# Where the router's features of a recurrence stage are made: VectorE, or ScalarE and GpSimd

## The chip, the cores and the metric

One NeuronCore of one Trainium2 chip runs the whole program. The metric is the device time of one execution in microseconds, lower is better. Before the change it is 8120.26 us (median of three runs, 8118.91 to 8121.44).

Names of engines as in the profile: PE is TensorE (PEld its weight loads), DVE is VectorE, ACT is ScalarE, POOL is GpSimd, SP is SyncE with its DMA queue.

## What is computed

Four layers are applied to x of shape (2, 4096, 512), each added to its input: a state-space layer, a dense layer, a gated linear recurrence with 8 heads of 64, and a routed spline layer. Only the third and the start of the fourth matter here:

```python
# third layer: decaying state per head
state = (1.0 - w_t)[..., :, None] * state + k_t[..., :, None] * v_t[..., None, :]
out = einsum('bhd,bhde->bhe', r_t, state)
x3 = x + out @ Wo.T

# fourth layer: norms twice, then routes by signs
z  = layernorm(x3)
xf = (z - mean(z)) * rsqrt(var(z) + 1e-5) * ln_gamma + ln_beta
tile_scores = sign(xf) @ tile_sigs.T       # 64 tiles of 8 features, in 8 clusters
tile_idx    = argmax over the tiles of the best cluster
x_slice     = the 8 values of xf that belong to tile_idx
```

Both norms together are one: with m the mean of x3 and s the joint factor, xf = (x3 - m) * s * gamma + beta. These xf, one row of 512 per token, are called the features below.

## The kernel before

All is in float32. Five stages follow one another: `pre_phase`, `scan_phase`, `mid_phase`, `core_phase`, `final_phase`. The change touches `core_phase` alone, the recurrence stage. It works through 64 items of 128 tokens (32 for each of the two sequences, taken in alternation: `par` is the sequence, `m` the place in it). Within an item the recurrence is done in parallel form: sub-blocks of 8 tokens, joined in a tree of four levels.

Each engine has its own program, a list of pieces run by `pipelined`. In one turn t an engine runs each piece of its list once, in the order of the list, for item t + lead. Engines keep no common clock; they are held together by `Count` semaphores: `c.inc(ins)` counts a finished instruction of an item, `c.wait(eng, item, n)` waits until n of that item are done, `c.wait_all` until all are. No planner orders anything: the lists are the order. For the turn of lead 1 (item i = t + 1) they are:

- DVE (L1349): `state` (L1270: four state updates; L1276: x3 = x + y from PSUM), `norms` (L1280 to L1286: mean, variance, ve), `limits` (L1348, item t), `centred` (L1292, L1295: the factors rt, by a Newton step on POOL's root; L1297, L1298: the features), `decays` (L1312, L1314: sixteen products for item t + 4, each of an SBUF operand with one in PSUM), `route` (L1333 to L1340: scores, best tile, one-hot oh), `spread_scores` (L1325, item t + 3).
- POOL (L1238): `more_keys` (item t + 3), `root` (L1160: ve to the power -0.5), `last_keys` (t + 3: L1175, L1183 twice, then L1219 twice, kl and ql), `totals` (L1167), `flip` (L1230: signs times the tiles' signs), `keys` (L1191 to L1183, item t + 4, waits for `decays`), `pick` (L1236: features times one-hot).
- ACT (L1417): `own_reads` (L1370, L1371, item t + 4), `pad_keys` (L1378), `attended` (L1385: two copies ats; L1387: k8t; item t + 2), `scores` (L1396, item t + 3), `kept` (L1403 to L1406: the layer's output x3 + z into xo), `signs` (L1412), `outputs` (L1416, item t + 2).
- PE (L1520): `tree` (L1460, item t + 2, waits for `spread_scores`), `turn_keys` (L1468), `products` (L1479, item t + 3), `reads` (L1489, L1495), `turn_scores` (L1502), `sums` (L1512), `outputs` (L1518).
- SP (L1139): loads of a, k, r five items ahead, of v and x three ahead, and the store of xo.

The features have one buffer, xf [128, 512]. They are written by DVE, read by ACT for the signs and by POOL in `pick`:

```python
after.link(dve, dve.scalar_tensor_tensor(out=xf[:], in0=x3[:], scalar=mv[:, 0:1], in1=gam[:], op0=ALU.subtract, op1=ALU.mult))
after.inc(dve.scalar_tensor_tensor(out=xf[:], in0=xf[:], scalar=rt[:, 1:2], in1=bet[:], op0=ALU.mult, op1=ALU.add))
```

Chain for one item: DVE `norms`, POOL `root`, DVE `centred`, ACT `signs`, POOL `flip`, DVE `route`, POOL `pick`, DVE `limits` one turn later.

Of the kernel before, what the change touches and what calls it, by code (L numbers as in the profile page):

```python
# [3 lines left out]
ALU = mybir.AluOpType  # L4
# [984 lines left out]
def core_phase(nc, D, H, L, a_s, k_s, r_s, v_s, x2_s, wo_d, gam_d, bet_d, slopes_d, key_row_d, mask_d, hmask_d, ident_d, x3_s, oh_out, xs_out):  # L989
# [15 lines left out]
    with ExitStack() as ctx:  # L1005
# [27 lines left out]
        mask = sb("mask", [P, P]); hmask = sb("hmask", [P, P]); ident = sb("ident", [P, P]); heads = sb("heads", [P, 2, P // 8])  # L1033
        st = sb("st", [P, 6]); mv = sb("mv", [P, 2]); ve = sb("ve", [P, 2]); half_neg = sb("half_neg", [P, 2]); r0 = sb("r0", [P, 2]); rt = sb("rt", [P, 2]); tmp = sb("tmp", [P, 2]); nve = sb("nve", [P, 2])
        keep = sb("keep", [P, 2])
# [31 lines left out]

        act_a = Count(sem("act_a"), 4)

        after = Count(sem("after"), 17)  # L1070
        S_STATE, S_X3, S_VE, S_RT, S_XF, S_OH = 1, 2, 6, 11, 13, 17

        pool_b = Count(sem("pool_b"), 3)

        routed = Count(sem("routed"), 1)

        act_r = Count(sem("act_r"), 5)
        R_KEPT = 4

# [68 lines left out]
        def _(pool):  # L1148
# [5 lines left out]
            pool.wait_ge(zeroed, 7)  # L1154
            pool.wait_ge(sgn_ready, 1)

            def root(i, par, m):
# [54 lines left out]
            def last_keys(i, par, m):  # L1212
                last = 8
                for l in range(3, LEVELS):
                    last = wider(i, par, l, last)
                pool_a.wait(pool, i, last)
                for kind, src, dst in ((1, rk[:, par, SUB], steps(kl[:, par])), (0, first[:, par, 0:SUB], ql[:, par])):
                    f = far[LEVELS][:, kind * C:(kind + 1) * C].rearrange("p (o c) -> p o c", o=1).broadcast_to([P, SUB, C])
                    pool_a.inc(pool.tensor_tensor(dst, src, f, ALU.mult))  # L1219

            def totals(i, par, m):
                totaled.begin(i)

                after.wait(pool, i - 2, S_STATE)
                totaled.inc(join(LEVELS - 1, par))

            def flip(i, par, m):
# [4 lines left out]
            def pick(i, par, m):  # L1232
# [4 lines left out]
                                              oh[:, bass.ds(par * (L // P) + m, 1), :].rearrange("p o (n e) -> p (o n) e", e=1).broadcast_to([P, NT, 8]), ALU.mult))  # L1237
            pipelined(pool, ITEMS, [(3, more_keys), (1, root), (3, last_keys), (3, totals), (1, flip), (4, keys), (1, pick)])  # L1238

        @block.vector  # L1240
        def _(dve):
# [46 lines left out]
            def centred(i, par, m):  # L1288
                pool_b.wait(dve, i, 1)
                after.wait(dve, i, S_VE + 1)  # L1290
                for e in range(2):
                    after.inc(dve.tensor_scalar(tmp[:, e:e + 1], r0[:, e:e + 1], r0[:, e:e + 1], nve[:, e:e + 1], ALU.mult, ALU.mult))  # L1292
                after.wait(dve, i, S_VE + 3)
                for e in range(2):
                    after.inc(dve.tensor_scalar(rt[:, e:e + 1], tmp[:, e:e + 1], 1.5, r0[:, e:e + 1], ALU.add, ALU.mult))  # L1295
                after.wait(dve, i, S_RT)
                after.link(dve, dve.scalar_tensor_tensor(out=xf[:], in0=x3[:], scalar=mv[:, 0:1], in1=gam[:], op0=ALU.subtract, op1=ALU.mult))  # L1297
                after.inc(dve.scalar_tensor_tensor(out=xf[:], in0=xf[:], scalar=rt[:, 1:2], in1=bet[:], op0=ALU.mult, op1=ALU.add))  # L1298

# [17 lines left out]
            def spread_scores(i, par, m):  # L1317
                spread.begin(i)
                pe_a.wait_all(dve, i)

                act_a.wait(dve, i - 1, 2)
                shape = [P, Q, NI, SUB]
# [6 lines left out]
            def route(i, par, m):  # L1329
                at = lambda t: t[:, bass.ds(par * (L // P) + m, 1), :].rearrange("p o n -> p (o n)")  # L1330

                pool_b.wait(dve, i, 2)
                dve.tensor_reduce(ts[:], sg[:], AX.X, ALU.add).then_inc(key_read, 1)  # L1333
# [18 lines left out]
        def _(act):  # L1352
# [27 lines left out]
            def attended(i, par, m):  # L1380
                act_a.begin(i)

                pe_b.wait(act, i, B_TREE)
                for h2 in range(2):
                    act_a.inc(act.copy(ats[:, h2], at_ps[:, h2]))  # L1385
                pe_b.wait(act, i, B_KEYS)
                act_a.inc(act.copy(k8t[:], kt_ps))  # L1387

# [8 lines left out]

            def kept(i, par, m):
                act_r.begin(i)

                act.wait_ge(x3_out[par], (m + 1) * 16)
                after.wait(act, i, S_RT)
                act_r.inc(act.activation(keep[:, 0:1], rt[:, 0:1], ACT.Identity, bias=1.0))  # L1403
# [4 lines left out]
            def signs(i, par, m):  # L1408

                after.wait(act, i, S_XF)  # L1410
                act.wait_ge(key_read, i + 1)
                act_r.inc(act.activation(signs_of, by_tile(xf), ACT.Sign))  # L1412

            def outputs(i, par, m):
                pe_b.wait(act, i, B_OUT)
                act_a.inc(act.copy(ot[:], o_ps))  # L1416
            pipelined(act, ITEMS, [(4, own_reads), (3, pad_keys), (2, attended), (3, scores), (1, kept), (1, signs), (2, outputs)])  # L1417

        @block.tensor
        def _(pe):  # L1420
# [62 lines left out]
            def reads(i, par, m):  # L1483

                pool_a.wait_all(pe, i)
                after.wait(pe, i - 2, S_STATE)
                act_a.wait(pe, i, 3)
                for q in range(Q):
                    pe.matmul(o_ps[:, q, :], s[:, par, q, :], steps(ql[:, par, :, q * NI:(q + 1) * NI]), start=(q == 0), stop=True, skip_group_check=True)  # L1489
                act_a.wait(pe, i, 2)  # L1490
                pe.wait_ge(ins_b[par], (m + 1) * 32)
# [13 lines left out]
            def sums(i, par, m):  # L1505

                act_a.wait(pe, i, 3)
                after.wait(pe, i - 1, S_STATE)
# [300 lines left out]
```

## Time and profile before

| what | value |
|---|---|
| median of three runs | 8120.26 us (8118.91 to 8121.44) |
| the profiled execution | 8123.72 us |
| its span in the profile | 8121.9 us |
| busy over the span | PE 7231.2 (89%), DVE 6749.7 (83%), ACT 4754.7 (59%), POOL 5820.1 (72%) |
| L1297 and L1298, 64 each | first features at 6722.8 us, last at 7868.0 us |

The profile is of one execution. Its times count from the span's start. In a timeline each line has the start, the duration, the engine, the line of the program, the operation with output <- inputs, and in brackets how long the engine sat idle before it and which instruction ended that. Durations contain the tail of an instruction, which the next one on the same engine overlaps by some 0.05 us. PEclk is the granted share of TensorE's full clock.

### The profile page before, as it was taken

To read this page: it belongs to the slowest core of one execution; us is meant where nothing else is said; L and a number is where in the kernel's file an instruction comes from. 1 tells how busy PE (TensorE), PEld (TensorE's weight loads), DVE (VectorE), ACT (ScalarE), POOL (GpSimd) and SP (SyncE) were. 2 spreads that over 40 slices of the span, in tenths; PEclk is the share of its full clock that TensorE was granted. 3 is DMA by queue.
4 is the path that set the end of the run, shared out by engine and by line. 5 is a ranking of instruction groups with operands and counts; after the bars stand their busy time and mean duration, and the time that the engine had idled before them with its cause. 6 is when DMAs were issued, how large, how long until landed. Compare 5 with 4: busy or idle time off the path is not lost. (4 is left out here: it accounts for less than half of the span.)

```text
span 8121.9 us, 217686 instructions
## 1 busy us (share of the span) xinstructions
PE 7231.2 (89%) x74510; PEld 5288.9 (65%) x74510; DVE 6749.7 (83%) x8153; ACT 4754.7 (59%) x10889; POOL 5820.1 (72%) x3400
## 2 busy tenths in 40 slices
PE   8799999999999999999999999799999988888863
PEld 4577777777777777777777777444444435555542
DVE  7799999999999999999999999423232329999976
ACT  7778778778887787888877877211111113333320
POOL 1499999999999999999999999300000006777644
PEclk9999999999999999999999999899999998888875
DMA  6500000000000000000000000212211222222224
GB/s 208 157 1 16 16 8 8 16 13 4 16 16 0 16 16 0 16 16 0 17 16 0 16 5 0 81 74 92 88 72 72 93 77 88 88 85 86 86 84 155
DMA packets 198187, 389.94 MB, mean 48 GB/s; under 512 B 26224, under 2 KB 51888, under 8 KB 186544
## 3 DMA queue, kind: packets, MB, share of 16 engines
q1 hardware_dynamic: 189088, 370.45, 13.7%
q10 hardware_dynamic: 8976, 17.83, 0.6%
q8 instruction: 80, 1.31, 0.1%
q14 instruction: 43, 0.35, 0.0%
HBM read 208.52 MB, written 179.70 MB: 48 GB/s over the span
## 5 line engine op out<-in xcount | busy, mean ns | idle before, releaser
L494 POOL TENSOR_TENSOR scan_hc<-scan_h,scan_cb 128x1024 f32<-128x1024 f32 x2048 | 4776.3, 2367 | 103.0 <-PE scan_y L617 81.7
L659 DVE TENSOR_TENSOR_SCAN scan_h<-scan_a,scan_carry,scan_u 128x512 f32<-128x512 f32 x4096 | 4800.3, 1256 | 15.8 <-PE scan_u L606 8.0
L553 ACT ACTIVATE scan_a<-scan_dt,scan_aneg 128x512 f32<-128x512 f32 x4096 | 2658.3, 708 | 7.4 <-ACT scan_yo L533 7.4
L606 PE MATMUL scan_u<-scan_dg,scan_v 64*128 64x128 f32 x32768 | 2379.8, 285 | 313.3 <-DVE scan_h L659 269.5
L606 PEld LDWEIGHTS scan_u<-scan_dg,scan_v 64*128 64x128 f32 x32768 | 1990.4, 187 | 793.2 <-DVE scan_h L659 556.2
L617 PE MATMUL scan_y<-scan_ident,scan_hc 128*128 128x128 f32 x16408 | 2251.8, 280 | 14.3 <-ACT scan_yo L533 9.9
L617 PEld LDWEIGHTS scan_y<-scan_ident,scan_hc 128*128 128x128 f32 x16408 | 1758.2, 140 | 272.9 <-ACT scan_yo L533 15.7
L524 ACT ACTIVATE scan_dg<-scan_half,scan_bt 128x64 f32<-128x64 f32 x4096 | 1139.0, 341 | 5.9 <-DVE scan_onward L645 5.2
L164 POOL TENSOR_TENSOR mid_r<-mid_ve,mid_half_neg 128x4 f32<-128x4 f32 x32 | 32.4, 1012 | 1288.0 <-DVE mid_ve L132 797.7
L545 ACT ACTIVATE scan_carry<-scan_h,scan_onward 128x4 f32 (+1 forms) x1008 | 302.9, 300 | 934.3 <-DVE scan_h L659 934.2
L809 DVE TENSOR_TENSOR mid_x<-mid_x,mid_pa 128x512 f32<-128x512 f32 x64 | 44.1, 688 | 432.8 <-PE mid_pa L918 432.8
L865 ACT ACTIVATE mid_rt<-mid_pb 128x512 f32<-128x512 f32 x64 | 38.2, 598 | 610.1 <-PE mid_pb L929 610.1
L798 DVE TENSOR_TENSOR mid_x<-mid_x,mid_pa 128x512 f32<-128x512 f32 x64 | 44.0, 688 | 318.3 <-PE mid_pa L900 318.3
L1385 ACT COPY core_ats<-core_at_ps 128x512 f32<-128x512 f32 x128 | 68.7, 590 | 397.3 <-PE core_at_ps L1460 397.3
L1460 PE MATMUL core_at_ps<-core_first,core_rk 64*8 64x8 f32 x4096 | 90.8, 174 | 201.5 <-DVE core_at_ps L1325 197.0
L1314 DVE TENSOR_TENSOR core_rk<-core_rr,core_ak_ps 128x128 f32<-128x128 f32 (+7 forms) x512 | 260.3, 508 | 0.0
L860 ACT ACTIVATE mid_at<-mid_pb,mid_bwn 128x512 f32<-128x512 f32 x64 | 44.0, 687 | 345.3 <-PE mid_pb L929 320.4
L929 PE MATMUL mid_pb<-mid_xnt,mid_wr 128*128 128x512 f32 x512 | 223.9, 595 | 20.7 <-DVE mid_kt L821 20.7
L1518 PE MATMUL core_y_ps<-core_wo,core_ot 128*128 128x512 f32 x512 | 236.8, 605 | 0.2 <-ACT core_ot L1416 0.2
L1460 PEld LDWEIGHTS core_at_ps<-core_first,core_rk 64*8 64x8 f32 x4096 | 70.9, 91 | 252.1 <-issue 252.1
L826 DVE COPY mid_vv<-mid_pb 128x512 f32<-128x512 f32 x64 | 44.3, 692 | 227.0 <-PE mid_pb L954 227.0
L1312 DVE TENSOR_TENSOR core_rr<-core_rr,core_ak_ps 128x128 f32<-128x128 f32 (+6 forms) x448 | 212.9, 475 | 20.1 <-ACT core_rr L1371 10.7
(212 smaller groups left out, 7246.5 us busy)
## 6 DMA issues: line engine op xcount, KB each, us to landing
scratch_y<-scan_yo ACTq DMA_DIRECT2D x17, 1024.0 KB, 4.3
pre_x<-in_x SPq DMA_DIRECT2D x16, 1024.0 KB, 5.7
scratch_dt<-pre_dt SPq DMA_DIRECT2D x16, 1024.0 KB, 5.8
scratch_vr<-pre_vr SPq DMA_DIRECT2D x16, 1024.0 KB, 4.7
scan_dt<-scratch_dt SPq DMA_DIRECT2D x16, 1024.0 KB, 5.3
scan_v<-scratch_vr SPq DMA_DIRECT2D x32, 512.0 KB, 7.6
mid_yr<-scratch_y SPq DMA_DIRECT2D x16, 1024.0 KB, 7.0
mid_x<-in_x SPq DMA_DIRECT2D x16, 1024.0 KB, 8.2
```

Source lines behind the costliest of these rows:

```text
L494: pool.tensor_tensor(hc[:, q].rearrange("p n (r j) -> p n r j", j=P), h[:, q].rearrange("p n (r j) -> p n r j", j=P), cb[:, bass.ds(b * NS ...
L524: last = act.activation(dg[:, buf, k, :, n], half[:], ACT.Identity, scale=bt[:, par, k, bass.ds(first + n, 1)])
L545: act.activation(carry[:, q0:q0 + 2, bass.ds(first, 2)], h[:, q0:q0 + 2, :, T - 1], ACT.Identity, scale=keep[:, bass.ds(c, 1)]).then_inc(s ...
L553: ins = act.activation(a[:, q, n, :], dt[:, par, q, :], ACT.Exp, scale=aneg[:, q, bass.ds(m * 2 + n, 1)])
L606: mm = pe.matmul(u_ps[:, q % 2, g, k * HP:(k + 1) * HP, :], v[row, par, k, q, :], dg[row, buf, k], start=True, stop=True)
L617: mm = pe.matmul(y_ps[:, j, q * P:(q + 1) * P], hc[:, q, n, j * P:(j + 1) * P], ident[:], is_transpose=True, start=first and n == 0, stop= ...
L659: ins = dve.tensor_tensor_scan(h[:, q, n, :], a[:, q, n, :], u_ps[:, q % 2, :, :, n].rearrange("p g t -> p (g t)"), carry[:, q, bass.ds(m ...
L929: mm = pe.matmul(pb[:, o, :], weight[:, q, o * P:(o + 1) * P], src[:, q, :], start=(q == 0), stop=(q == Q - 1))
L1312: decayed = chain.inc(dve.tensor_tensor((rr[:, j - 1] if j else first[:, par])[:, j:W], rr[:, j, j:W], ak_ps[:, 0, j:j + 1, :].broadcast_t ...
L1314: chain.inc(dve.tensor_tensor(rk[:, par, j:W, j, :], rr[:, j, j:W], ak_ps[:, 1, j:j + 1, :].broadcast_to(shape), ALU.mult))
L1460: mm = pe.matmul(at_ps[lo:lo + rows, h2, q, at + n:at + 2 * n], keys, reads, start=False, stop=True, skip_group_check=True, tile_position= ...
L1518: mm = pe.matmul(y_ps[:], ot[:, q, :], wo[:, q, :], start=(q == 0), stop=(q == Q - 1))
```

## The change

The features are made in three steps on two engines: ACT computes (x3 - m) * s as an activation with scale s and bias `shift` = -m * s; POOL multiplies by gam and adds bet, both in place. DVE makes only `shift`. On POOL the new piece `features` stands between `last_keys` and the two products of L1219, which become a piece of their own, `ends_keys`. On ACT the new piece `normed` stands ahead of `attended`, and `attended` copies k8t first. `signs` waits for POOL in place of DVE. POOL also waits once, at the stage's start, for the constants. Counts and waits are renumbered.

```diff
-        after = Count(sem("after"), 17)
-        S_STATE, S_X3, S_VE, S_RT, S_XF, S_OH = 1, 2, 6, 11, 13, 17
-        pool_b = Count(sem("pool_b"), 3)
+        A_K8T, A_ATS = 1, 3
+        after = Count(sem("after"), 16)
+        S_STATE, S_X3, S_VE, S_RT, S_SHIFT, S_OH = 1, 2, 6, 11, 12, 16
+        pool_b = Count(sem("pool_b"), 5)
+        B_XF, B_FLIP = 3, 4
-        act_r = Count(sem("act_r"), 5)
-        R_KEPT = 4
+        act_r = Count(sem("act_r"), 6)
+        R_XN, R_KEPT = 1, 5
...
             def last_keys(i, par, m):
                 last = 8
                 for l in range(3, LEVELS):
                     last = wider(i, par, l, last)
-                pool_a.wait(pool, i, last)
+
+            def ends_keys(i, par, m):
+                pool_a.wait(pool, i, A_TREE - 2)
                 for kind, src, dst in (...):
...
+            def features(i, par, m):
+                act_r.wait(pool, i, R_XN)
+                pool_b.inc(pool.tensor_tensor(xf[:], xf[:], gam[:], ALU.mult))
+                pool_b.wait(pool, i, B_XF - 1)
+                pool_b.inc(pool.tensor_tensor(xf[:], xf[:], bet[:], ALU.add))
...
-            pipelined(pool, ITEMS, [(3, more_keys), (1, root), (3, last_keys), (3, totals), (1, flip), (4, keys), (1, pick)])
+            pipelined(pool, ITEMS, [(3, more_keys), (1, root), (3, last_keys), (1, features), (3, ends_keys), (3, totals), (1, flip), (4, keys), (1, pick)])
...
                 after.wait(dve, i, S_RT)
-                after.link(dve, dve.scalar_tensor_tensor(out=xf[:], in0=x3[:], scalar=mv[:, 0:1], in1=gam[:], op0=ALU.subtract, op1=ALU.mult))
-                after.inc(dve.scalar_tensor_tensor(out=xf[:], in0=xf[:], scalar=rt[:, 1:2], in1=bet[:], op0=ALU.mult, op1=ALU.add))
+                after.inc(dve.tensor_scalar(shift[:], mv[:, 0:1], rt[:, 1:2], -1.0, ALU.mult, ALU.mult))
...
             def attended(i, par, m):
                 act_a.begin(i)
-                pe_b.wait(act, i, B_TREE)
+                pe_b.wait(act, i, B_KEYS)
+                act_a.inc(act.copy(k8t[:], kt_ps))
                 for h2 in range(2):
                     act_a.inc(act.copy(ats[:, h2], at_ps[:, h2]))
-                pe_b.wait(act, i, B_KEYS)
-                act_a.inc(act.copy(k8t[:], kt_ps))
...
+            def normed(i, par, m):
+                act_r.begin(i)
+                pool_b.wait_all(act, i - 1)
+                after.wait(act, i, S_SHIFT)
+                act_r.inc(act.activation(xf[:], x3[:], ACT.Identity, bias=shift[:], scale=rt[:, 1:2]))
+
             def kept(i, par, m):
-                act_r.begin(i)
                 act.wait_ge(x3_out[par], (m + 1) * 16)
-                after.wait(act, i, S_RT)
...
             def signs(i, par, m):
-                after.wait(act, i, S_XF)
+                pool_b.wait(act, i, B_XF)
...
-            pipelined(act, ITEMS, [(4, own_reads), (3, pad_keys), (2, attended), (3, scores), (1, kept), (1, signs), (2, outputs)])
+            pipelined(act, ITEMS, [(4, own_reads), (3, pad_keys), (1, normed), (2, attended), (3, scores), (1, kept), (1, signs), (2, outputs)])
```

## Rows read from the trace of the kernel before

**Rows 1.** Busy time by stretch: mid stage, then recurrence stage; columns in the header.

```profile
core 0: us, PE busy (x) PEld busy (x) DVE busy (x) ACT busy (x) POOL busy (x), PEclk, DMA share, GB/s
5900.00:6100.00 200.00, 194.25 (x534) 91.48 (x533) 57.04 (x124) 29.36 (x47) 17.91 (x8) 1.00 0.20 73
7000.00:7300.00 300.00, 244.17 (x5104) 166.50 (x5104) 287.49 (x657) 113.62 (x247) 209.08 (x311) 0.87 0.26 85
```

**Rows 2.** Timeline of DVE, one turn: start us, us, engine, line, operation [idle before].

```profile
7192.31 1.11 DVE L1270 SCALAR_TENSOR_TENSOR core_s<-core_s,core_total,core_su_ps 128x128 f32<-128x128 f32 x4
...
7196.77 0.34 DVE L1295 TENSOR_SCALAR core_rt<-core_tmp,core_r 128x1 f32<-128x1 f32 x2
7197.14 1.25 DVE L1297 SCALAR_TENSOR_TENSOR core_xf<-core_x,core_mv,core_gam 128x512 f32<-128x512 f32 x1
7198.43 1.65 DVE L1298 SCALAR_TENSOR_TENSOR core_xf<-core_xf,core_rt,core_bet 128x512 f32<-128x512 f32 x1
7200.00 0.28 DVE L1312 TENSOR_TENSOR core_rr<-core_rr,core_ak_ps 128x128 f32<-128x128 f32 x1
...
7206.90 0.74 DVE L1333 TENSOR_REDUCE core_ts<-core_sg 128x64 f32<-128x576 f32 x1
...
7210.55 1.11 DVE L1270 SCALAR_TENSOR_TENSOR core_s<-core_s,core_total,core_su_ps 128x128 f32<-128x128 f32 x4
```

**Rows 3.** Timeline of POOL, the same turn.

```profile
7197.12 0.72 POOL L1183 TENSOR_TENSOR core_qr<-core_first,core_far 128x256 f32<-128x256 f32 x1
7197.81 1.73 POOL L1219 TENSOR_TENSOR core_kl<-core_rk,core_far 128x512 f32<-128x512 f32 x1
7199.49 1.73 POOL L1219 TENSOR_TENSOR core_ql<-core_first,core_far 128x512 f32<-128x512 f32 x1
7201.18 0.20 POOL L1167 TENSOR_TENSOR core_total<-core_joint 128x4 f32<-128x4 f32 x1
7201.62 1.20 POOL L1230 TENSOR_TENSOR core_sg<-core_sg,core_sgn 128x512 f32<-128x512 f32 x1 [0.25 <-ACT core_sg L1412]
7207.14 0.30 POOL L1191 COPY core_own<-core_first 128x64 f32<-128x64 f32 x1 [4.32 <-DVE core_rk L1314]
...
7209.92 1.08 POOL L1236 TENSOR_TENSOR core_pr<-core_xf,core_oh 128x512 f32<-128x512 f32 x1
```

**Rows 4.** Timeline of ACT, the same turn.

```profile
7196.60 1.07 ACT L1385 COPY core_ats<-core_at_ps 128x512 f32<-128x512 f32 x2 [5.87 <-PE core_at_ps L1460]
...
7200.21 0.82 ACT L1406 ACTIVATE core_xo<-core_x,core_keep 128x512 f32<-128x512 f32 x1
7200.93 0.62 ACT L1412 ACTIVATE core_sg<-core_xf 128x512 f32<-128x512 f32 x1
```

**Rows 5.** Timeline of POOL, then DVE, in the stage's first turn.

```profile
6725.75 1.28 POOL L1219 TENSOR_TENSOR core_ql<-core_first,core_far 128x512 f32<-128x512 f32 x1
...
6731.17 1.20 POOL L1230 TENSOR_TENSOR core_sg<-core_sg,core_sgn 128x512 f32<-128x512 f32 x1 [3.98 <-ACT core_sg L1412]
...
6735.74 1.11 DVE L1270 SCALAR_TENSOR_TENSOR core_s<-core_s,core_total,core_su_ps 128x128 f32<-128x128 f32 x4
```

**Rows 6.** Two lines' instructions: count, ns min/median/max, first and last start.

```profile
L1219 POOL TENSOR_TENSOR core_kl<-core_rk,core_far x64: 1273/1730/1747, 6696.4 to 7837.0; 128x512 f32<-128x512 f32 x64
...
L1297 DVE SCALAR_TENSOR_TENSOR core_xf<-core_x,core_mv,core_gam x64: 750/1253/1265, 6722.8 to 7868.0; 128x512 f32<-128x512 f32 x64
```

**Rows 7.** Timeline of DVE: first and last of 60 turn starts.

```profile
6754.36 1.11 DVE L1270 SCALAR_TENSOR_TENSOR core_s<-core_s,core_total,core_su_ps 128x128 f32<-128x128 f32 x4
...
7831.02 1.11 DVE L1270 SCALAR_TENSOR_TENSOR core_s<-core_s,core_total,core_su_ps 128x128 f32<-128x128 f32 x4
```

**Rows 8.** Timeline of PE, a turn with a stretch at the lower clock.

```profile
7265.64 0.37 PE L1460 MATMUL core_at_ps<-core_first,core_rk 64*8 64x8 f32 x16 [3.67 <-DVE core_at_ps L1325]
...
7269.75 1.12 PE L1468 MATMUL core_y_ps<-core_ident,core_kl 128*128 128x128 f32 x4
...
7277.65 3.70 PE L1518 MATMUL core_y_ps<-core_wo,core_ot 128*128 128x512 f32 x8
```

More of the change, by code:

```diff
@@ L1033, in core_phase @@
         mask = sb("mask", [P, P]); hmask = sb("hmask", [P, P]); ident = sb("ident", [P, P]); heads = sb("heads", [P, 2, P // 8])
-        st = sb("st", [P, 6]); mv = sb("mv", [P, 2]); ve = sb("ve", [P, 2]); half_neg = sb("half_neg", [P, 2]); r0 = sb("r0", [P, 2]); rt = sb("rt", [P, 2]); tmp = sb("tmp", [P, 2]); nve = sb("nve", [P, 2])
+        st = sb("st", [P, 6]); mv = sb("mv", [P, 2]); ve = sb("ve", [P, 2]); half_neg = sb("half_neg", [P, 2]); r0 = sb("r0", [P, 2]); rt = sb("rt", [P, 2]); tmp = sb("tmp", [P, 2]); nve = sb("nve", [P, 2]); shift = sb("shift", [P, 1])
         keep = sb("keep", [P, 2])
@@ L1155, in _ @@
             pool.wait_ge(sgn_ready, 1)
+            pool.wait_ge(consts, 128)
             def root(i, par, m):
@@ L1319, in spread_scores @@
                 pe_a.wait_all(dve, i)
-                act_a.wait(dve, i - 1, 2)
+                act_a.wait(dve, i - 1, A_ATS)
                 shape = [P, Q, NI, SUB]
@@ L1330, in route @@
                 at = lambda t: t[:, bass.ds(par * (L // P) + m, 1), :].rearrange("p o n -> p (o n)")
-                pool_b.wait(dve, i, 2)
+                pool_b.wait(dve, i, B_FLIP)
                 dve.tensor_reduce(ts[:], sg[:], AX.X, ALU.add).then_inc(key_read, 1)
@@ L1486, in reads @@
                 after.wait(pe, i - 2, S_STATE)
-                act_a.wait(pe, i, 3)
+                act_a.wait(pe, i, A_K8T)
                 for q in range(Q):
                     pe.matmul(o_ps[:, q, :], s[:, par, q, :], steps(ql[:, par, :, q * NI:(q + 1) * NI]), start=(q == 0), stop=True, skip_group_check=True)
-                act_a.wait(pe, i, 2)
+                act_a.wait(pe, i, A_ATS)
                 pe.wait_ge(ins_b[par], (m + 1) * 32)
@@ L1505, in sums @@
             def sums(i, par, m):
-                act_a.wait(pe, i, 3)
+                act_a.wait(pe, i, A_K8T)
                 after.wait(pe, i - 1, S_STATE)
```

## The prediction

> **What bounds the kernel now.** I read the windows of busy time first, then the timelines of DVE, POOL and ACT over one turn, then the forms of single lines. The recurrence stage (features from 6722.8 to 7868.0 [rows 6]) is some 1,150 of the 8,122 us; in it DVE is busy 287.49 of 300 us, PE 244, POOL 209 and ACT 114 [rows 1]. The reader should see one engine without room and three with some. DVE's timeline shows the same: from 7192.31 to 7210.55 its instructions follow one another [rows 2]. So a turn lasts as long as DVE's list. From 6754.36 to 7831.02 there are 59 turns of 18.25 us [rows 7]: that is P, and 0.1 us of P is worth 5.9 us. I count the parts of a turn from DVE's first instruction of it, 7192.31 = 0: the features begin at 4.83 (L1297) and 6.12 (L1298), the sixteen multiplications of `decays` at 7.69, `route` at 14.59 (L1333), and the next turn at 18.24 [rows 2].
>
> POOL in the same turn is idle for 4.32 us before L1191 [rows 3]. Its two 128x512 key products (L1219) last 1.73 us each, just beside DVE's two feature instructions. Yet the shortest of that line is 1.273 us, and one in the first turn, begun after the features, took 1.28 [rows 5, 6]. DVE's L1297 likewise takes 1.25 us but at its shortest 0.75 [rows 2, 6]. So these pairs hold each other up: the 0.46 us that each key product has over 1.27 is the features' doing.
>
> **Part 1: off DVE.** L1297 and L1298 go: 4.83 to 7.69, 2.86 us. One 128x1 product for `shift` comes in; two of that size take 0.34 us [rows 2], so 0.20, to 5.03. The multiplications then begin at 5.03, last 6.90 (7200.00 to 7206.90) and end at 11.93.
>
> **Part 2: onto ACT.** The activation has the form of L1406, a 128x512 Identity with bias and scale from tiles: 0.82 us [rows 4]. A handoff costs 0.07 (L1412 ends at 7201.55, L1230 begins at 7201.62) [rows 3, 4]. It runs from 5.10 to 5.92. Its other waits, for `pick` of the item before, ended a turn earlier. Behind it on ACT stand `attended`, `scores`, `kept` and `signs`, now from 7196.60 to 7201.55, 4.95 us or 4.29 to 9.24 [rows 4]. They begin 1.6 later, when the activation is done and PE has turned the keys (5.2, at the lower clock about 5.5 [rows 8]); so the signs are ready by 10.9. Of `attended` the copy k8t now comes first. PE's `reads` want it first as well, and the two ats copies (1.07 us [rows 4]) only for their second half, so I cost the swap at nothing; without that cover PE would lose at most the 0.6 of one copy, out of the slack of part 4.
>
> **Part 3: onto POOL.** Two 128x512 products. The trace before has none with two plain rows; the nearest are L1236, 1.08 us, and L1230, 1.20, and above them L1219 beside DVE, 1.73 [rows 3]. I take L1230's 1.20, since its two inputs are full rows too. POOL has finished L1183 at 5.53 and idles until ACT's result: first product 5.99 to 7.19, handoff 0.07, second 7.26 to 8.46. The key products follow: they have no feature instruction beside them any more, so 1.27 each less 0.05 overlap, to 10.90. The total's product (0.20 [rows 3]) and a handoff put `flip` at about 11.2, just behind the signs. The new wait of `features` delays only the key products, which PE wants a turn later.
>
> **Part 4: what is late next.** `flip` takes 1.20 and then `route` can begin: 12.45, half a microsecond after the multiplications are over (11.93). DVE waits 0.5 there. What comes after `flip` is read in the first turn, where DVE waited for it as well: `flip` began at 6731.17 and the next turn at 6735.74, 4.57 us later [rows 5]. So P = 11.2 + 4.57 = 15.77. POOL's rest of the turn (L1191 to L1236 and `more_keys`) keeps its distance to the turn's start, because there too it began right behind `flip`; so the next `root` finds POOL free as now. PE is busy 244.17 x 18.25 / 300 = 14.9 us per turn [rows 1]; a long one, with a stretch at the lower clock, goes from 7265.64 to 7281.35, 15.7 [rows 8]. It starts 0.3 after DVE's turn does (7265.64 against 6754.36 + 28 x 18.25), so it ends at 16.0 at worst and its next turn begins at 16.1. It fits, barely. Its tree, 4.1 us of that (to 7269.75), ends at 4.4, before the multiplications, which wait for it, begin at 5.03. The change issues and moves no DMA; the loads and the store of a turn stay the same, so their 85 GB/s and 0.26 share [rows 1] grow by 18.25 / 15.77 to 98 GB/s and 0.30, which I cost at nothing: they are issued three and five items ahead. The norm ahead of the features is as before: DVE's `norms`, POOL's `root`, which finds POOL idle, and DVE's L1292 and L1295.
>
> **Sum.** 59 turns x (18.25 - 15.77) = 146.3 us off. The turn before them, 6735.74 to 6754.36 [rows 5, 7], was partly held by PE: I count half, 1.3 off. In the last turn nothing hides the longer way from shift to signs: 0.20 + 0.82 + 2 x 1.20 + three handoffs = 3.6 in place of 2 x 0.75 [rows 6], 2.1 on. Net 145.5. The profiled execution took 8123.7 (span 8121.9, 1.8 around it), so 7978.2 for it; the median of the runs shown, 8120.3, is 3.4 lower: **7975 us**. Bounds: products at 1.08 give P 15.53 (7961), at 1.73 P 16.83 (8037). The floor is DVE without any wait: 11.93, plus 3.27 from `route` to the next turn (4.57 less 1.20 and a handoff of 0.1), P 15.20, or 7941.
>
> **The clock.** At 97% busy in the mid stage TensorE had 1.00 of its clock, at 81% here 0.87, a mix of the 2.4 and 1.2 GHz levels [rows 1]. In the new turn PE would be busy over 90% of the time, so I expect the share to rise. It is worth nothing to the sum while PE has slack.
>
> **Rivals.** *DVE stays the bound*: products at 1.08 or overlapped better, no wait at `route`; P 15.2 to 15.5, 7941 to 7959. Against it: POOL's chain must lose 0.5 us. *The lock moves, it does not go*: the key products stay at 1.73 because something else of DVE's holds them up, P + 0.92 = 16.69, 8029. For it: the 1.73 is nearly constant. Against: the 1.28 of the first turn fell beside the multiplications [rows 5]. The Trainium skill (Perfetto Trace Analysis, Optimizing Scalar/DVE Operations) speaks against the change as a whole: VectorE and GpSimd share an SBUF read port, so moving work between those two might not help. By that rule this rival is the likely one; I keep it low for the row of 1.28. Its page SBUF — State Buffer (Who interferes with whom) narrows it: a VectorE instruction with two SBUF inputs and a GpSimd instruction that reads SBUF block each other fully. The 0.46 us agree; and since the multiplications read one operand from PSUM, by this rule my main case holds.
>
> *PE becomes the bound*: the stretches at the lower clock stay and every turn is the long one, P 16.1, 7994. *Slower than before*: POOL's four large products (4.9 us in a row, 5.99 to 10.90) hold up DVE's multiplications, which start at the same time. Fully blocked, these end at 16.83, P = 20.1, 8230. It decides from 3.05 us of blocking per turn on (18.25 - 15.20). Against it: the first of them, 0.28 us from 7200.00, runs wholly beside an L1219 that ends at 7201.22 and does not wait for it [rows 2, 3]. *The wait takes all*: the way over three engines costs 2.4 more than I add up, and the time is as before.
>
> **How the numbers follow.** Main case 0.68, DVE bound 0.12, lock moved 0.08, PE bound 0.06, as before 0.03, slower 0.03. The prediction is the main case. The range runs from the floor, 7941, to the lock's rival, 8030; it takes in PE's and all but the highest price of the products. A measurement of this kernel tells 0.2%, 16 us, from no change. Faster 0.94, same 0.03, slower 0.03.
>
> **What would show it.** In the profile after: DVE idle about 0.5 us before L1333's reduction, released by POOL's `flip`; L1219 at 1.27; two new POOL groups at about 1.2; POOL waiting some 0.4 for ACT's activation; turn starts 15.8 apart; a granted clock over 0.9. I am wrong if L1219 stays at 1.7, if L1312 and L1314 grow, or if DVE waits for PE at L1312 or L1325.

## The result and the profile after

| | before | after |
|---|---|---|
| median, four runs each on one chip | 8119.59 us (8112.90 to 8121.44) | 7977.44 us (7975.57 to 7979.41) |
| ratio | | 0.9827 [0.9815, 0.9838] |
| profiled execution, its span | 8123.72, 8121.9 us | 7975.57, 7973.8 us |
| turn of the recurrence stage | 18.25 us | 15.845 us |
| busy in the span: DVE, POOL | 6749.7, 5820.1 us | 6579.7, 5927.6 us |
| granted clock, whole span | 0.957 | 0.966 |

The change is faster by 142.2 us; forecast were 145. The second stretch of [rows 1], 7000 to 7300, after the change (same columns):

```profile
7000.00:7300.00 300.00, 277.68 (x6003) 187.90 (x6003) 278.82 (x740) 138.93 (x303) 274.64 (x399) 0.93 0.30 99
```

DVE is down from 287.49 to 278.82 us, POOL up from 209 to 274.64, PE up from 244 to 277.68: three engines are now at 91 to 93%. The granted clock is up from 0.87 to 0.93. One turn on DVE, to be held against [rows 2]:

```profile
7191.33 1.11 DVE L1283 SCALAR_TENSOR_TENSOR core_s<-core_s,core_total,core_su_ps 128x128 f32<-128x128 f32 x4
...
7195.75 0.34 DVE L1308 TENSOR_SCALAR core_rt<-core_tmp,core_r 128x1 f32<-128x1 f32 x2
7196.12 0.21 DVE L1310 TENSOR_SCALAR core_shift<-core_mv,core_rt 128x1 f32<-128x1 f32 x1
7196.60 0.29 DVE L1324 TENSOR_TENSOR core_rr<-core_rr,core_ak_ps 128x128 f32<-128x128 f32 x1 [0.26 <-issue]
...
7202.84 0.75 DVE L1326 TENSOR_TENSOR core_rk<-core_rr,core_ak_ps 128x576 f32<-128x576 f32 x1
7203.80 0.75 DVE L1345 TENSOR_REDUCE core_ts<-core_sg 128x64 f32<-128x576 f32 x1 [0.21 <-POOL core_sg L1243]
...
7204.84 0.45 DVE L1349 SCALAR_TENSOR_TENSOR core_key<-core_cl,core_ts 128x64 f32<-128x64 f32 x1
...
7205.69 0.36 DVE L1352 TENSOR_SCALAR core_oh<-core_key,core_kmax 128x64 f32 x1 [0.15 <-DVE core_kmax L1351]
...
7207.17 1.11 DVE L1283 SCALAR_TENSOR_TENSOR core_s<-core_s,core_total,core_su_ps 128x128 f32<-128x128 f32 x4
```

The same turn on POOL, against [rows 3]:

```profile
7196.15 0.73 POOL L1186 TENSOR_TENSOR core_qr<-core_first,core_far 128x256 f32<-128x256 f32 x1
7197.26 1.28 POOL L1236 TENSOR_TENSOR core_xf<-core_xf,core_gam 128x512 f32<-128x512 f32 x1 [0.38 <-ACT core_xf L1414]
7198.62 1.28 POOL L1238 TENSOR_TENSOR core_xf<-core_xf,core_bet 128x512 f32<-128x512 f32 x1
7199.86 1.30 POOL L1225 TENSOR_TENSOR core_kl<-core_rk,core_far 128x512 f32<-128x512 f32 x1
7201.11 1.27 POOL L1225 TENSOR_TENSOR core_ql<-core_first,core_far 128x512 f32<-128x512 f32 x1
...
7202.50 1.19 POOL L1243 TENSOR_TENSOR core_sg<-core_sg,core_sgn 128x512 f32<-128x512 f32 x1
7203.76 0.29 POOL L1194 COPY core_own<-core_first 128x64 f32<-128x64 f32 x1
...
7204.35 0.85 POOL L1186 TENSOR_TENSOR core_kc<-core_rk,core_own 128x256 f32<-128x256 f32 x1
```

and on ACT, against [rows 4]:

```profile
7196.37 0.81 ACT L1414 ACTIVATE core_xf<-core_x,core_shift,core_rt 128x512 f32<-128x512 f32 x1 [6.62 <-DVE core_shift L1310]
...
7200.66 0.64 ACT L1428 ACTIVATE core_sg<-core_xf 128x512 f32<-128x512 f32 x1
```

All key products of the stage (count, ns min/median/max), against [rows 6]:

```profile
L1225 POOL TENSOR_TENSOR core_kl<-core_rk,core_far x64: 1272/1292/1309, 6691.2 to 7691.0; 128x512 f32<-128x512 f32 x64
```

Counted from the turn's start at 7191.33: the activation runs from 5.04 to 5.85, the first product begins at 5.93, `flip` at 11.17, DVE's `route` at 12.47 after 0.21 us idle, and the next turn at 15.84. The key products take 1.29 us where they took 1.73. Two things were not on my list. DVE stands idle 0.26 us before its first multiplication (7196.60), with no engine named. And the key of `route` (L1349; L1337 before) takes 0.45 us where it took longer before:

```profile
7207.92 0.74 DVE L1337 SCALAR_TENSOR_TENSOR core_key<-core_cl,core_ts 128x64 f32<-128x64 f32 x1
```

**Where the 148.1 us between the two spans are.** 58 turns (6763.52 to 7682.51) at 15.845 in place of 18.25: 139.4. The three before them took 18.88, 17.54 and 16.76 us, against 19.01, 18.62 and 18.25: 2.7 (before the change DVE began the stage's first turn at 6716.73; the starts of the next two are in [rows 5, 7]). The end of the program from the last long turn on is 0.4 us longer. That leaves 6.4 us: the stage's first turn began at 6710.34 in place of 6716.73, before anything that was changed, and repeated runs of one kernel differ by as much (6716.34 in the changed kernel's second profile, below). The first turns gained little because DVE waited for PE's tree, 1.56 us in the first turn and 1.18 in the third. PE had begun that first tree 2.76 us after DVE began the turn (6713.10), where it is 0.32 to 0.35 in later turns. From 6680 to 6702, while PE was mostly idle or waiting, its granted clock was 0.50, the 1.2 GHz level; from 6706 to 6714 it was 1.00. How much of the delay is the clock's, no run shows. DVE in the first turn after the change:

```profile
6710.34 1.11 DVE L1283 SCALAR_TENSOR_TENSOR core_s<-core_s,core_total,core_su_ps 128x128 f32<-128x128 f32 x4
...
6718.65 0.29 DVE L1324 TENSOR_TENSOR core_rr<-core_rr,core_ak_ps 128x128 f32<-128x128 f32 x1 [1.56 <-PE core_at_ps L1476]
...
6729.22 1.11 DVE L1283 SCALAR_TENSOR_TENSOR core_s<-core_s,core_total,core_su_ps 128x128 f32<-128x128 f32 x4
```

### The profile page after: what moved, and what is told of

The parts are those of the page before. It is cut to its first block and busy times, and to the rows that moved or that the text cites. A ratio compares the mean times of both kernels' runs of the same rounds, so it can differ in the third digit from the quotient of the medians.

```text
span 7973.8 us, 217784 instructions
## 1 busy us (share of the span) xinstructions
PE 7210.3 (90%) x74510; PEld 5270.5 (66%) x74510; DVE 6579.7 (83%) x8089; ACT 4783.8 (60%) x10953; POOL 5927.6 (74%) x3528
## 5 line engine op out<-in xcount | busy, mean ns | idle before, releaser
L617 PEld LDWEIGHTS scan_y<-scan_ident,scan_hc 128*128 128x128 f32 x16408 | 1757.4, 140 | 272.9 <-ACT scan_yo L533 15.7
L1414 ACT ACTIVATE core_xf<-core_x,core_shift,core_rt 128x512 f32<-128x512 f32 x64 | 52.1, 814 | 425.4 <-DVE core_shift L1310 425.4
L1326 DVE TENSOR_TENSOR core_rk<-core_rr,core_ak_ps 128x128 f32<-128x128 f32 (+7 forms) x512 | 263.4, 514 | 0.0
L1324 DVE TENSOR_TENSOR core_rr<-core_rr,core_ak_ps 128x128 f32<-128x128 f32 (+6 forms) x448 | 215.9, 482 | 38.0 <-PE core_at_ps L1476 12.6
L929 PE MATMUL mid_pb<-mid_xnt,mid_wxw 128*128 128x512 f32 x512 | 225.7, 594 | 0.9 <-DVE mid_vv L826 0.9
L918 PE MATMUL mid_pa<-mid_w,mid_ht 128*128 128x512 f32 x512 | 224.1, 596 | 2.1 <-ACT mid_ht L852 2.1
```

What stands on the lines that cost most here:

```text
L617: mm = pe.matmul(y_ps[:, j, q * P:(q + 1) * P], hc[:, q, n, j * P:(j + 1) * P], ident[:], is_transpose=True, start=first and n == 0, stop= ...
L918: mm = pe.matmul(pa[:, j, :], ht[:, q, j * P:(j + 1) * P], w["w0"][:, q, :], start=(q == 0), stop=(q == Q - 1))
L929: mm = pe.matmul(pb[:, o, :], weight[:, q, o * P:(o + 1) * P], src[:, q, :], start=(q == 0), stop=(q == Q - 1))
L1324: decayed = chain.inc(dve.tensor_tensor((rr[:, j - 1] if j else first[:, par])[:, j:W], rr[:, j, j:W], ak_ps[:, 0, j:j + 1, :].broadcast_t ...
L1326: chain.inc(dve.tensor_tensor(rk[:, par, j:W, j, :], rr[:, j, j:W], ak_ps[:, 1, j:j + 1, :].broadcast_to(shape), ALU.mult))
```

## The experiments

Twelve kernels ran, each beside the kernel before on the same chip; the text calls them by the first part of their names (e1, e2 and so on). Unless it says otherwise, a diff is against the changed kernel. "Turn" is the mean over some 30 turns of the profile. The changed kernel, run again as the yardstick:

> The changed kernel once more, as the yardstick for the runs beside it: ratio to the kernel before 0.982 to 0.983, turn 15.84 us.

Measured: 7980.86 us (7977.19 to 7982.98), ratio 0.9828 [0.9815, 0.9842], turn 15.844.

### What the features cost DVE before: work or waiting?

e1: in the kernel before, the two feature instructions are replaced by two reductions that read the same row of x with one input.

```diff
-                after.link(dve, dve.scalar_tensor_tensor(out=xf[:], in0=x3[:], scalar=mv[:, 0:1], in1=gam[:], ...))
-                after.inc(dve.scalar_tensor_tensor(out=xf[:], in0=xf[:], scalar=rt[:, 1:2], in1=bet[:], ...))
+                after.link(dve, dve.bn_stats(st_a[:], x3[:]))
+                after.inc(dve.bn_stats(st_b[:], x3[:]))
```

> The kernel before, with DVE's two feature instructions (two SBUF inputs each, 1.25 and 1.65 us) replaced by two BATCH_NORM_STATS of x3 (one SBUF input each, 0.69 us); the features are left out. My theory, that the two features and POOL's two key products hold each other up: the key products (L1219 before) fall from 1.73 to about 1.27 us each although POOL's list is untouched, the two reductions fill 0.85 + 0.65 = 1.5 us of DVE's turn in place of 2.86, and the turn falls from 18.25 to 16.9 us, some 80 us in all. So 1.36 of the 2.86 us that the change took off DVE were waiting for the port. Rival (the key products are slow by themselves or because of DVE's multiplications): they stay at 1.7.

Measured: 8030.89 us (two runs), ratio 0.9892 [0.9863, 0.992], turn 16.73. POOL's key products in it:

```profile
L1219 POOL TENSOR_TENSOR core_kl<-core_rk,core_far x64: 1274/1288/1308, 6694.4 to 7744.3; 128x512 f32<-128x512 f32 x64
```

1.29 us, with POOL's own list untouched. So the two engines did hold each other up. On DVE the two reductions fill 1.34 us, and the turn is 1.52 shorter. The shortest of the two feature instructions take 0.75 us each, 1.5 together, so of their 2.86 us some 1.36 were waiting. The reductions have one input less, but they also write only six elements per partition; e1 by itself does not tell these two apart. The multiplications do: they write full rows to SBUF with one input in SBUF and one in PSUM, and they take no longer beside POOL's products (below, under the other rivals).

### One product less, one more

e2: without the second of the two products.

```diff
-                pool_b.wait(pool, i, B_XF - 1)
-                pool_b.inc(pool.tensor_tensor(xf[:], xf[:], bet[:], ALU.add))
```

> The changed kernel, without the addition of bet on POOL (left out of the computation). My theory: POOL's chain from the activation to flip sets the turn, but only by DVE's 0.22 us idle before route; with one product (1.36 us with its handoff) less, DVE's own list sets it: turn 15.84 - 0.22 = 15.6 us, some 13 us less in all, DVE's idle before route gone. Rival (POOL is the bound throughout): turn 14.5 us, 80 us less.

Measured: 7977.94 us (two runs), ratio 0.9826 [0.9798, 0.9855], turn 15.85: nothing gained. DVE in `route`:

```profile
7189.72 0.74 DVE L1343 TENSOR_REDUCE core_ts<-core_sg 128x64 f32<-128x576 f32 x1
...
7190.75 0.75 DVE L1347 SCALAR_TENSOR_TENSOR core_key<-core_cl,core_ts 128x64 f32<-128x64 f32 x1
...
7191.92 0.35 DVE L1350 TENSOR_SCALAR core_oh<-core_key,core_kmax 128x64 f32 x1 [0.17 <-DVE core_kmax L1349]
```

DVE's idle before L1343, the first line, is gone as forecast, but the key after it (L1347) is at 0.75 us again, where the changed kernel had 0.45. What the end of the wait gave, the key took. POOL in the same turn:

```profile
7189.96 0.30 POOL L1194 COPY core_own<-core_first 128x64 f32<-128x64 f32 x1 [1.17 <-DVE core_rk L1324]
...
7190.57 0.85 POOL L1186 TENSOR_TENSOR core_kc<-core_rk,core_own 128x256 f32<-128x256 f32 x1
```

POOL's piece `keys`, which waits for DVE's last multiplication, now waits for it openly. In the changed kernel `keys` (L1194, 7203.76) begins 0.17 us after the end of the last multiplication (L1326, 7203.59), the same distance as here, in e7 and before the change. So there too the multiplications released it, although `flip` had ended only 0.07 us before. In both kernels L1186 begins 13.02 to 13.03 us into the turn, and that is why they have the same turn.

e3: a third product, by a row of ones, is put in.

```diff
                 pool_b.inc(pool.tensor_tensor(xf[:], xf[:], bet[:], ALU.add))
+                pool_b.wait(pool, i, B_XF - 1)
+                pool_b.inc(pool.tensor_tensor(xf[:], xf[:], ones_row[:], ALU.mult))
```

> The changed kernel, with a third product of the same size on the features on POOL (by a row of ones). My theory: it lies wholly on the chain that sets the turn: turn 15.84 + 1.28 + 0.08 = 17.2 us, 80 us more than the changed kernel, and all of it as DVE's idle time before route (0.22 becomes 1.6). Rival (PE or DVE sets the turn and POOL has room): less than half of that.

Measured: 8059.85 us, ratio 0.9924 [0.9902, 0.9947], turn 17.12, 1.28 more. The first instruction of `route`:

```profile
7197.65 0.75 DVE L1348 TENSOR_REDUCE core_ts<-core_sg 128x64 f32<-128x576 f32 x1 [1.53 <-POOL core_sg L1245]
```

A product more costs 1.28 us, one less gives nothing: the changed kernel stands within 0.1 us of where the two ways to POOL's `keys`, over `flip` and over the multiplications, are equally long. In e3, e5, e6 and e9 `flip` is the last of the two, and the next turn then begins 4.55 to 4.57 us after its start; in the changed kernel it is 4.67.

### The order on ACT and on POOL

e4: the order of ACT's copies alone, in the kernel before (k8t ahead of ats, counts renumbered as in the change):

> The kernel before, with ACT's attended in the changed order alone (k8t ahead of the two ats copies). My theory: worth nothing by itself, since DVE's list sets the turn: turn 18.25 us, within 5 us of the kernel before. Rival (part of the 2.41 us per turn comes from this order, through PE's reads): faster by over 16 us.

Measured: 8118.92 us against 8118.03, ratio 1.0001 [0.9992, 1.001], turn 18.26. It is worth nothing by itself.

e5: the activation stands behind `attended` and `scores`.

```diff
-            pipelined(act, ITEMS, [..., (1, normed), (2, attended), (3, scores), (1, kept), (1, signs), (2, outputs)])
+            pipelined(act, ITEMS, [..., (2, attended), (3, scores), (1, normed), (1, kept), (1, signs), (2, outputs)])
```

> The changed kernel, with normed moved on ACT from ahead of attended to its old place, just ahead of kept. My theory: the activation then starts only after the scores' copies, 7.6 us after the turn's start in place of 5.04; POOL waits with nothing else to do, since its list is in order, and the turn grows by all of it: about 18.3 us, some 150 us more than the changed kernel, no faster than the kernel before. Rival (the place on ACT doesn't matter because POOL's key products or DVE's multiplications cover it): within 20 us of the changed kernel.

Measured: 8130.25 us, ratio 1.0014 [1.0002, 1.0025], turn 18.20. The activation's place in ACT's list is worth the whole gain: with the work moved off DVE all the same, the kernel is no faster than before.

e6: the key products stand ahead of the features on POOL.

```diff
-            pipelined(pool, ITEMS, [..., (3, last_keys), (1, features), (3, ends_keys), (3, totals), (1, flip), ...])
+            pipelined(pool, ITEMS, [..., (3, last_keys), (3, ends_keys), (1, features), (3, totals), (1, flip), ...])
```

> The changed kernel, with POOL's ends_keys ahead of features in place of behind. My theory: POOL fills its 0.4 us wait for the activation with key products, but then the signs on ACT (0.62 us and two handoffs) stand bare between the second product and flip: flip starts at about 11.45 us of the turn in place of 11.17, the turn is 16.1 us, some 17 us more than the changed kernel. Rival (the order on POOL is worth nothing, its sum decides): turn within 0.1 us of 15.84, or shorter by the 0.38 us of the wait that goes, 15.6.

Measured: 7987.03 us, ratio 0.9835 [0.9822, 0.9849], turn 15.98: 6 us more than the yardstick in time, within the noise of both, but 0.13 us more in every turn. `flip` does start later, at 11.4; `route` gives part of it back, since its key takes 0.33 us here. My 17 us were too many.

### What bounds the changed kernel

e7: the signs ahead of `kept` on ACT, and `flip` ahead of the second key product on POOL.

```diff
-            pipelined(act, ITEMS, [..., (3, scores), (1, kept), (1, signs), (2, outputs)])
+            pipelined(act, ITEMS, [..., (3, scores), (1, signs), (1, kept), (2, outputs)])
...
-            pipelined(pool, ITEMS, [..., (1, features), (3, ends_keys), (3, totals), (1, flip), (4, keys), (1, pick)])
+            pipelined(pool, ITEMS, [..., (1, features), (3, end_keys), (1, flip), (3, end_reads), (3, totals), (4, keys), (1, pick)])
```

> An attempt at a faster kernel: the changed kernel with signs ahead of kept on ACT, and on POOL flip between the two key products, so that nothing stands between features and flip but one key product. My theory: flip ends about 1.2 us earlier, before DVE's multiplications do (12.2); DVE's 0.22 us idle before route goes and DVE's list alone sets the turn: 15.6 us, 13 us less than the changed kernel. Rival (PE, 14.7 to 15.7 us per turn, is already the bound next to it): the same as the changed kernel.

Measured: 7980.46 us, ratio 0.9828 [0.9815, 0.9842], turn 15.845: nothing. It looks as if the rival held, that PE is the bound (e8 and e12 below, at turns of 15.23 and 15.35 with PE's list unchanged, put it out). Its DVE in `route`:

```profile
7189.53 0.74 DVE L1349 TENSOR_REDUCE core_ts<-core_sg 128x64 f32<-128x576 f32 x1
...
7190.56 0.75 DVE L1353 SCALAR_TENSOR_TENSOR core_key<-core_cl,core_ts 128x64 f32<-128x64 f32 x1
...
7191.74 0.34 DVE L1356 TENSOR_SCALAR core_oh<-core_key,core_kmax 128x64 f32 x1 [0.17 <-DVE core_kmax L1355]
```

and its POOL:

```profile
7190.38 0.86 POOL L1186 TENSOR_TENSOR core_kc<-core_rk,core_own 128x256 f32<-128x256 f32 x1
7191.19 0.84 POOL L1186 TENSOR_TENSOR core_qr<-core_first,core_own 128x256 f32<-128x256 f32 x1
```

DVE waits for nothing at 7189.53, and the key takes 0.75. It ends, at 7191.31, within 0.07 us of POOL's first L1186 (7191.24), and the one-hot (L1356, 7192.08) within 0.05 of the second (7192.03). Over the 32 turns from 6900 to 7400 the two distances are 0.06 to 0.09 and 0.04 to 0.06 us, and in the kernel before they are the same.

e8: e7, with the four waits that stood at the head of `decays` set behind `norms`.

```diff
+            def ready(i, par, m):
+                dve.wait_ge(ins_a[par], (m + 1) * 48)
+                pool_a.wait_freed(dve, i)
+                padded.wait_freed(dve, i)
+                diagonal.wait_all(dve, i)
...
-            pipelined(dve, ITEMS, [(1, state), (1, norms), (0, limits), (1, centred), (4, decays), ...])
+            pipelined(dve, ITEMS, [(1, state), (1, norms), (4, ready), (0, limits), (1, centred), (4, decays), ...])
```

> As the attempt with signs first, and four of the five waits of decays on DVE (loads, POOL, padding, ACT's copies) put ahead of limits in place of just before the multiplications. My theory: the 0.25 us idle before the first multiplication, which the trace puts down to no other engine, is DVE's sequencer working through five waits with nothing long left to hide them; moved behind norms they are hidden by limits: turn 15.4 us, 12 us less again (25 less than the changed kernel). Rival (that gap is a wait for PE's tree, as some of the trace's lines have it): the gap and the turn stay.

Measured: 7944.25 us (7942.09 to 7949.49), ratio 0.9787 [0.9773, 0.98], turn 15.23: 36.6 us less than the yardstick, more than my theory had. DVE in `route`:

```profile
7186.62 0.74 DVE L1349 TENSOR_REDUCE core_ts<-core_sg 128x64 f32<-128x576 f32 x1
...
7187.65 0.23 DVE L1353 SCALAR_TENSOR_TENSOR core_key<-core_cl,core_ts 128x64 f32<-128x64 f32 x1
...
7188.28 0.36 DVE L1356 TENSOR_SCALAR core_oh<-core_key,core_kmax 128x64 f32 x1 [0.15 <-DVE core_kmax L1355]
```

and its POOL:

```profile
7187.71 0.88 POOL L1186 TENSOR_TENSOR core_kc<-core_rk,core_own 128x256 f32<-128x256 f32 x1
7188.54 0.84 POOL L1186 TENSOR_TENSOR core_qr<-core_first,core_own 128x256 f32<-128x256 f32 x1
```

The key takes 0.23. From the first reduction to the next turn `route` and `spread_scores` take 3.13 us (7186.62 to 7189.75) where e7 needs 3.67. Is it the waits, or the place of these instructions against POOL's? Three kernels tell. First e9, the waits alone, in the changed kernel:

> The changed kernel, with four of the five waits of decays moved ahead of limits, and nothing else. Theory A (DVE's sequencer is late; POOL's chain sets the turn): the 0.25 us idle before the first multiplication goes, and comes back as idle before route, 0.2 to 0.45 us; turn 15.84 us, within 5 us of the changed kernel. Rival (the early waits are what made the attempt e8 faster): turn 15.3 to 15.6 us, 15 to 36 us less.

Measured: 7989.43 us, ratio 0.9842 [0.9828, 0.9855], turn 16.02. Two instructions of its DVE:

```profile
7195.92 0.69 DVE L1360 TENSOR_REDUCE core_xs<-core_pr 128x512 f32 x1 [0.34 <-issue]
...
7205.06 0.75 DVE L1345 TENSOR_REDUCE core_ts<-core_sg 128x64 f32<-128x576 f32 x1 [0.58 <-POOL core_sg L1243]
```

The gap before the first multiplication is gone, and one of 0.34 stands before `limits`, with no engine named either. So it is DVE's own queue at work on the waits: it moves with them and is not hidden. It costs 8.6 us here, and neither theory had that: the gap now stands ahead of `shift`, on the way to `flip`, which starts at 11.41 in place of 11.17. It can't be what made e8 faster.

In e10, the key of e7 is made by an instruction with one SBUF input, the maximum and the one-hot read ts, and the clusters' part of the score is left out:

```diff
-                after.link(dve, dve.scalar_tensor_tensor(out=by_cluster(key), in0=cl[...], scalar=256.0, in1=by_cluster(ts), ...))
+                after.link(dve, dve.bn_stats(st_k[:], ts[:]))
```

> The attempt e7 (signs first), with the key product of route (L1353 there, two SBUF inputs, 128x64, 0.75 us in e7 and 0.22 at its shortest) replaced by a BATCH_NORM_STATS of ts, one SBUF input; the clusters' part of the score is left out. Theory B, formed after e2 and e7 gained nothing: once DVE no longer waits for flip, POOL's key product L1186 is running when DVE's comes, and it waits for the port, 0.5 us, which gives back what the end of the wait had brought. Then the turn falls by 0.4 to 0.55 us, to about 15.35, some 30 us less than e7. Rival (something else, PE or POOL's list, holds the turn at 15.84): within 5 us of e7.

Measured: 7980.78 us, ratio 0.9829 [0.9814, 0.9844], turn 15.84: by its number, a miss. Its DVE:

```profile
7193.24 0.23 DVE L1353 BATCH_NORM_STATS2 core_st_k<-core_ts 128x6 f32<-128x64 f32 x1
...
7193.89 0.87 DVE L1356 TENSOR_SCALAR core_oh<-core_ts,core_kmax 128x64 f32 x1 [0.17 <-DVE core_kmax L1355]
```

and its POOL:

```profile
7193.07 0.85 POOL L1186 TENSOR_TENSOR core_kc<-core_rk,core_own 128x256 f32<-128x256 f32 x1
7193.87 0.84 POOL L1186 TENSOR_TENSOR core_qr<-core_first,core_own 128x256 f32<-128x256 f32 x1
```

The key is down to 0.23, and the one-hot behind it, a TENSOR_SCALAR, has grown from 0.34 to 0.87. It was asked for at 7193.89, just after the second L1186 had begun, and ended at 7194.76, when that one had. The wait is the same; another instruction bears it. In e8 the one-hot was asked for at 7188.28, inside the first L1186, and came through between the two. So I put the theory once more, with a kernel that touches only POOL's order in e7:

```diff
                 pool_a.inc(join(0, par))
+                pool_a.wait(pool, i, 2)
+                pool_a.inc(join(1, par))
                 pool_a.inc(half(1, 1, par))
                 pool_a.inc(half(1, 0, par))
-                pool_a.wait(pool, i, 2)
-                pool_a.inc(join(1, par))
```

> The attempt e7 (signs first), with one small product of POOL's keys (join(1), 0.23 us and a handoff) moved ahead of the two half products L1186, so that these start some 0.3 us later against DVE's route; DVE's program is e7's. Theory B, corrected after e10: with two POOL products back to back, DVE's two instructions of route that need the port (the key, L1353, and the one-hot, L1356) get it only when one of them is asked for before POOL's runs, or while the first of POOL's is still running; in e7 and e10 the last of them ends only with POOL's second product. Shifted by 0.3 us the key comes before the first product and the one-hot between the two: key 0.22 in place of 0.75, turn 15.3 to 15.4 us, some 28 us less than e7. Rival (e8's gain of 36 us came from the place of DVE's waits): turn 15.84, within 5 us of e7.

Measured: 7948.26 us (7944.76 to 7953.36), ratio 0.979 [0.9777, 0.9804], turn 15.35. Its DVE:

```profile
7201.95 0.74 DVE L1349 TENSOR_REDUCE core_ts<-core_sg 128x64 f32<-128x576 f32 x1
...
7202.98 0.25 DVE L1353 SCALAR_TENSOR_TENSOR core_key<-core_cl,core_ts 128x64 f32<-128x64 f32 x1
...
7203.66 0.36 DVE L1356 TENSOR_SCALAR core_oh<-core_key,core_kmax 128x64 f32 x1 [0.17 <-DVE core_kmax L1355]
```

and its POOL:

```profile
7202.93 0.23 POOL L1172 TENSOR_TENSOR core_joint<-core_joint 128x16 f32<-128x16 f32 x1
7203.11 0.85 POOL L1186 TENSOR_TENSOR core_kc<-core_rk,core_own 128x256 f32<-128x256 f32 x1
7203.92 0.84 POOL L1186 TENSOR_TENSOR core_qr<-core_first,core_own 128x256 f32<-128x256 f32 x1
```

The key (7202.98) begins ahead of POOL's first product (7203.11) and takes 0.25; the one-hot, asked for while that product runs, ends at 7204.02, just after it. With DVE's program unchanged, 0.5 us per turn are gained by a shift of POOL's two products of 0.3 us: the first begins 1.16 us after the first reduction of `route`, in e7 0.85. Both e8 and e12 beat the changed kernel and the kernel before. They were not run together in one kernel.

## Why the prediction was right, and where its steps were off

The time, 7977 against 7975, was right. The work moved and the waiting that went with it were as given; what sets the new turn was so only within 0.1 us, which is luck, and sizes partly made up for each other. Within the stage the change gave 141.7 us, 145.5 were added up.

- **What bounds the kernel**: held in the main. A reordering on ACT alone changed nothing (e4), and in e1 DVE's list and the turn became shorter by the same 1.52 us. But the list was not all work: besides the 1.36 us in the features, the key took 0.74 us before the change where its shortest took 0.22.
- **Part 1**: the removed stretch and `shift` (0.21) as said. Missed: 0.25 us of DVE's queue before the multiplications, which the features had covered. With it they end at 12.26, not 11.93, and it is their end that releases POOL's `keys`. It cost about 0.1 us per turn, some 6 us in all, by an estimate: by `flip` alone the turn would be 11.17 + 4.57 = 15.74.
- **Part 2**: 5.04 to 5.85 against 5.10 to 5.92. The signs were ready at 9.97, not 10.9: of the 4.95 us taken from the kernel before, 0.49 were a wait for PE before the second L1396. That the activation must stand ahead of `attended` was not priced in the prediction; e5 did, at the whole gain.
- **Part 3**: the products took 1.28 us, not the 1.20 of L1230: they have the length of a key product without DVE beside it. The key products fell to 1.29 as forecast, and e1 shows the cause. The Trainium skill's rule that a VectorE instruction with two SBUF inputs contends with a GpSimd one that reads SBUF (SBUF — State Buffer, Who interferes with whom) agrees with e1. The Trainium skill's general warning on moving work between these two engines (Perfetto Trace Analysis, Optimizing Scalar/DVE Operations) did not come true for the change as a whole. What stands behind the warning, that the two share a port, took back the gain in e2, e7 and e10.
- **Part 4**: `flip` at 11.17 against 11.2, the next turn 4.67 later, not 4.57; a turn of 15.84 against 15.77. DVE did wait for `flip`, 0.21 us and not 0.5, but that wait did not set the turn: without it (e2) the turn is the same. The prediction had `flip` last by 0.57 us per turn (15.77 against 15.20); measured, the way over the multiplications, POOL's `keys` and its two L1186 is the longer one by 0.1. PE ended at 14.7 to 15.7 in its turn and never held up a regular one, as the margin said.
- **The floor was wrong.** The prediction put DVE without a wait for `flip` at 15.20, taking 3.27 us from `route` to the next turn from the stage's first turn. That length belongs to a `route` that begins just after `flip`, when POOL's next products come late. As soon as DVE doesn't wait for `flip`, `route` meets them and takes 3.67 (e7), as in the kernel before (3.66). The rival "DVE stays the bound" with 7941 to 7959 therefore could not come by faster products alone: e2 had the shorter chain and stayed at 7978. Only a change of order between `route` and POOL's products, in which `route` takes 3.14 to 3.18, came near the floor: 7944 (e8) and 7948 (e12).
- **The other rivals**: the key products did not stay at 1.73; the multiplications were not blocked by POOL's products (the 448 of L1324 have a median of 0.481 us, those of L1312 had 0.475); the way over the three engines was as added up.
- **The sum**: 2.405 us per turn against 2.48, over 58 turns; the first three gave 2.7 against 2.48 for one regular turn and 1.3 for one; the end cost 0.4, not 2.1. Another 6.4 us of the difference of spans lie before the stage.

## What to carry to other kernels

Before work is moved off a full engine, look for a second length of its neighbours: if an instruction beside it is now and then much shorter, part of the load is waiting, and both engines gain when one of the two goes. In a list that is worked in order, price the place of each new piece, not its length alone; here the place was worth the whole gain. And when an experiment takes a wait away and nothing changes, read the durations behind it: what two engines cost each other in e2, e7 and e10 showed as a longer instruction, not as idle time. Idle time with an engine named before it need not be the wait that sets the turn.

## What the runs showed of the hardware that I had not expected

- A 128x64 DVE instruction of 0.22 us takes up to 0.75 beside POOL products of 0.85, and when the key has one SBUF input only, the wait passes to the one-hot behind it (0.34 to 0.87; e7, e10). Asked for while one POOL product runs, the one-hot ends 0.1 us after the start of the next (e8, e12); asked for 0.02 us after that one's start, it ends with it (e10).
- A TENSOR_SCALAR from SBUF to SBUF with 64 elements per partition waits in this way too, though it has but one full input (e10). The Trainium skill (SBUF — State Buffer, Who interferes with whom) names `tensor_scalar` too among the operations that can contend.
- Semaphore waits ahead of a DVE instruction, long fulfilled, cost time when only short instructions stand before them: 0.24 to 0.28 us with five of them ahead of the first multiplication (changed kernel), 0.34 to 0.44 with four of them set ahead of `limits` and its own (e8, e9).
- A POOL product of two plain 128x512 rows in float32 takes 1.28 us (L1236, L1238 of the changed kernel), and the key products with no DVE instruction of two SBUF inputs beside them the same (1.29).
